# Tile numbers of the source stage read in smaller register loads, ranks kept in PSUM, and two loops with a fixed first slot

## The reference

```
h = relu(layernorm(x));  x = x + L0(h)     # attention: softmax over the edges of each node, weighted sum
h = relu(layernorm(x))
msg = relu(concat(h[src], h[dst], edge_attr) @ W1 + b1)
x = x + segment_sum(msg @ W2 + b2, src)    # summed by source node
```

## Time and profile before

| what | value |
|---|---|
| three executions, median (lowest to highest) | 5747.75 us (5745.49 to 5753.77) |
| the profiled execution | 5751.72 us, span in the profile 5749.9 us |
| mean granted clock of PE | 0.931 of full speed |
| PE busy | 5123.7 us, 89% of the span |
| DVE busy | 3965.7 us, 69% |
| ACT busy | 2966.4 us, 52% |
| POOL busy | 3885.3 us, 68% |
| chain that ended last | PE 57%, DMA 11%, issue 11%, POOL 9%, DVE 8% |
| source stage | 4378 to 5710 us, 107 turns |

### The profile page before, as it was taken

The page is one execution under the profiler, slowest core; times in us unless marked ns, Lnnn a source line. Parts: engine busy times, 40 slices in busy tenths (PEclk is TensorE's granted clock), DMA queues, the critical chain, the costliest instruction groups (busy, mean ns, idle before and its releaser), DMA issues.

```text
span 5749.9 us, 159286 instructions
## 1 busy us (share of the span) xinstructions
PE 5123.7 (89%) x33692; PEld 4028.2 (70%) x33693; DVE 3965.7 (69%) x14408; ACT 2966.4 (52%) x8485; POOL 3885.3 (68%) x3713
## 2 busy tenths in 40 slices
PE   4888888888888876999999999999997999999999
PEld 3677777777777764777666666666665777777777
DVE  6778788888778776555555555555455888888887
ACT  3566566666666553333333333332224777777776
POOL 4777777777777774777777777777775545545543
PEclk6888888888889887999999999999998999999999
DMA  4522222222222244999989989889996999999997
GB/s 109 163 53 53 53 53 54 53 53 53 53 53 53 53 127 130 281 271 266 260 256 265 257 256 263 263 235 282 253 257 176 214 210 213 212 211 214 212 212 188
DMA packets 859989, 990.83 MB, mean 172 GB/s; under 512 B 307993, under 2 KB 663225, under 8 KB 859775
## 3 DMA queue, kind: packets, MB, share of 16 engines
q1 hardware_dynamic: 662494, 608.23, 40.8%
q0 software_dynamic: 190592, 378.22, 24.6%
q10 hardware_dynamic: 6816, 3.38, 0.2%
HBM read 726.65 MB, written 262.76 MB: 172 GB/s over the span
## 4 chain that ended last, share of the span: by engine, by line
PE 57%; DMA 11%; issue 11%; POOL 9%; DVE 8%; DVEq 2%; ACT 2%; POOLq 0%; ACTq 0%; SPq 0%
PE bank L1703 13%; PE bank L1536 9%; PE bank L1626 8%; PE bank L1693 7%; PE bank L1628 7%; DMA xr<-arena 7%; POOL arena L498 4%; POOL xr L546 4%; PE bank L1462 2%; DMA arena<-h_tab,arena 2%; DVE arena L1054 2%; DVE arena L944 2%; PE bank L1616 2%; PE bank L1684 1%; DVEq L250 1%
## 5 line engine op out<-in xcount | busy, mean ns | idle before, releaser
L498 POOL DMA_INDIRECT arena<-h_tab,arena x1612 | 1563.8, 970 | 553.4 <-issue 408.4
L546 POOL DMA_INDIRECT xr<-arena x1612 | 1580.3, 980 | 511.9 <-issue 351.5
L1536 PE MATMUL bank<-arena 128*128 128x136 f32 x6448 | 1316.8, 333 | 73.3 <-DVE arena L1054 8.4
L718 ACT ACTIVATE arena<-bank 128x256 f32<-128x256 f32 x1612 | 593.3, 385 | 1400.8 <-PE bank L1628 923.3
L560 POOL DMA_INDIRECT arena<-p_tab,arena x428 | 666.8, 1558 | 667.1 <-DMA arena<-p_tab,arena 441.3
L1626 PE MATMUL bank<-arena 128*128 128x256 f32 x3224 | 1030.4, 402 | 91.5 <-ACT arena L718 50.5
L1536 PEld LDWEIGHTS bank<-arena 128*128 128x128 f32 x6448 | 987.1, 215 | 159.0 <-DVE arena L1054 63.2
L625 ACT ACTIVATE arena<-bank 128x256 bf16<-128x256 bf16 x1612 | 615.2, 382 | 808.1 <-PE bank L1462 727.6
L1628 PE MATMUL bank<-arena 128*128 128x256 f32 x3224 | 976.5, 385 | 0.0
L1703 PE MATMUL bank<-arena 128*128 128x257 f32 x3424 | 898.2, 384 | 4.2 <-ACT arena L795 2.2
L1054 DVE TENSOR_TENSOR arena<-arena,bank 128x272 f32 x1612 | 692.1, 429 | 188.8 <-PE bank L1536 160.2
(11 more groups left out here) (255 smaller groups left out, 6477.1 us busy)
## 6 DMA issues: line engine op xcount, KB each, us to landing
arena<-xr SPq DMA_DIRECT2D x428, 516.0 KB, 4.0
arena<-q_tab SPq DMA_DIRECT2D x1612, 128.0 KB
arena<-in_edge_attr SPq DMA_DIRECT2D x61, 832.0 KB, 8.8
arena<-rel_tab SPq DMA_DIRECT2D x124, 224.0 KB
arena<-h_tab,arena POOLq DMA_INDIRECT x1612
xr<-arena POOLq DMA_INDIRECT x1612
arena<-rel_tab SPq DMA_DIRECT2D x124, 192.0 KB
xr<-arena SPq DMA_DIRECT2D x26, 516.0 KB
```

What stands on the lines that cost most here:

```text
L498: pool.indirect_dma_start(G[:, q, t, :], None, h_tab, bass.IndirectOffsetOnAxis(ap=idx[:, q, t:t + 1], axis=0)).then_inc(sem(f"gath{q}"), 16)
L546: pool.indirect_dma_start(xr, bass.IndirectOffsetOnAxis(ap=pos[:, q, t:t + 1], axis=0), Rb[:, t, :], None).then_inc(sem(f"scat{m}"), 16)
L1536: last = pe.matmul(PSB[3 + t % 2][:, k * H * MW:(k + 1) * H * MW], OH[:, (t + 2 * q) % 4, k * P:(k + 1) * P], flat(msg[:, t, :, :]), start ...
```

## The change

In the source stage PE and DVE read the tile numbers differently. DVE still uses `pbrow`, but reads 8 columns a turn and not 12, and 4 for what stands behind its last turn. PE gets a second copy of the table, `pbrow1`, shifted so that the number of pair g stands in column g + 1: it reads 4 columns at m = 0 and 4 at m = 4 of each turn, from columns that are a multiple of 4, and a single one behind the loop. `pbrow1` lies where the row `d0row` of the target stage lay; SP loads it after its last load of that stage, and PE and DVE wait for both copies.

In the target stage `rank` on DVE adds `run0` in place, in PSUM, and `own` reads PSUM and writes `t49`; the bank is given back to PE by `own`, and no longer by `rank`.

DVE's and ACT's loops of the source stage begin at slot 0 of a block.

```diff
+        pbrow1 = Region(WORDS - NB * RB)([NPAIR + 16], I32, 1)
...
-        def pair_bins(engine, i):
+        def pair_bins(engine, row, first, count):
             return nc.values_load_multi_w_load_instructions(
-                pbrow[0:1, bass.ds(i * SB, SB + 4)], engines=[engine], min_val=0, max_val=NT - 1,
+                row[0:1, bass.ds(first, count)], engines=[engine], min_val=0, max_val=NT - 1,
...
             load_windows(NB - 1, 1, part=NT - 1)
-
+            sp.dma_start(pbrow1[:, 1:1 + NPAIR], pb_tab[0:NPAIR].rearrange("(a n) -> a n", a=1)).then_inc(sem("pb_in"), 16)
             sp.wait_ge(sem("main_done"), T)
...
-            with act.Fori(1, NTURN) as i:
+            with nc.Fori(1, NTURN, engines=[ENG.Activation], head_slot={ENG.Activation: 0}) as i:
                 sources(i)
...
             def rank(r, m):
-                V.tensor_tensor(t49[:, lo:hi, :], PSB[5][:, 0:(hi - lo) * NT].rearrange("p (t b) -> p t b", b=NT),
-                                run0.unsqueeze(1).to_broadcast([P, hi - lo, NT]), ALU.add).then_inc(sem("rk_used"), 1)
+                v = PSB[5][:, 0:(hi - lo) * NT].rearrange("p (t b) -> p t b", b=NT)
+                V.tensor_tensor(v, v, run0.unsqueeze(1).to_broadcast([P, hi - lo, NT]), ALU.add).then_inc(sem("run_added"), 1)
             def own(r, s, m):
-                dve.wait_ge(sem("rk_used"), 3 * r + m + 1)
-                V.tensor_tensor(t49[:, lo:hi, :], t49[:, lo:hi, :], oh49[:, s, lo:hi, :], ALU.mult).then_inc(sem("own_ready"), 1)
+                dve.wait_ge(sem("run_added"), 3 * r + m + 1)
+                V.tensor_tensor(t49[:, lo:hi, :], PSB[5][:, 0:(hi - lo) * NT].rearrange("p (t b) -> p t b", b=NT),
+                                oh49[:, s, lo:hi, :], ALU.mult).then_inc(sem("rk_used"), 1)
             def reduced(r):
-                dve.wait_ge(sem("own_ready"), 3 * r + 3)
+                dve.wait_ge(sem("rk_used"), 3 * r + 3)
...
-            dve.wait_ge(sem("pb_in"), 16)
+            dve.wait_ge(sem("pb_in"), 32)
...
             def sources(i, first=False, last=False):                    # DVE
-                regs = pair_bins(ENG.DVE, i)
+                regs = pair_bins(ENG.DVE, pbrow, SB * i, SB)
...
-            with dve.Fori(1, NTURN - 1) as i:
+            with nc.Fori(1, NTURN - 1, engines=[ENG.DVE], head_slot={ENG.DVE: 0}) as i:
                 sources(i)
             sources(NTURN - 1, last=True)
-            regs = pair_bins(ENG.DVE, NTURN)
+            regs = pair_bins(ENG.DVE, pbrow, NPAIR, 4)
...
             def sources(i, first=False):                                # PE
-                regs = pair_bins(ENG.PE, i)
                 for m in range(SB):
+                    if m % 4 == 0:
+                        regs = pair_bins(ENG.PE, pbrow1, SB * i + m, 4)
                     turnp(SB * i + m, m)
                     if not (first and m < 1):
-                        source_rows(SB * i + m - 1, (m - 1) % SB, regs[m + 3], first)
+                        source_rows(SB * i + m - 1, (m - 1) % SB, regs[m % 4], first)
...
-            pe.wait_ge(sem("pb_in"), 16)
+            pe.wait_ge(sem("pb_in"), 32)
...
-            regs = pair_bins(ENG.PE, NTURN)
-            source_rows(NPAIR - 1, SB - 1, regs[3], False)
+            regs = pair_bins(ENG.PE, pbrow1, NPAIR, 1)
+            source_rows(NPAIR - 1, SB - 1, regs[0], False)
```

## The result

The changed kernel takes 5705.26 us (median of 4 runs, 5700.23 to 5709.14) beside 5750.76 us for the kernel before in the same rounds (4 runs, 5745.49 to 5761.07). The ratio is 0.9918 with a 95% interval of [0.9901, 0.9935]: 47 us less, between 37 and 57. The forecast was 51 us less.

The account below looks back on a forecast made before the run. PE was taken to bound the source stage, losing 0.74 us around each turn's end. Terms -60 + 10 - 2 + 1 = -51 us gave 5697 us from a median of 5747.75; range 5672 to 5733 us.

Parts of the forecast that it names:

- PE at the turn's end: Source stage: PE's register load at each turn's end falls from 0.85 to 0.28 us; -60 us (bounds -74 to 0).
- The rival of a fixed price: A register load costs mostly the same whatever its count and PE pays twice; about 5745 us, no change; chance 0.11.
- Second load at m = 4: PE's new mid-turn load needs 0.47 us and slack covers 0.61, so nothing lost; 45 us lost at 0.85 us.
- The rival on the slower side: PE's second load at m = 4 comes uncovered, from 0.63 us a load on; 5778 us; chance 0.07.
- DVE's load: DVE's register load at the source turn's end falls from 0.85 to 0.57 us; alone worth 0, taken as 0.
- Late turns: Source turns delayed by chunk loads cost 14 us; shorter turns cut the four-buffer ring's slack; 24 us, so +10 (0 to +40).
- The rival that the ring takes +35 us: Source stage's ring of chunk buffers takes part of the gain, late turns growing by 35 us; 5723 us; chance 0.18.
- Ranks: Target stage: rank kept in PSUM leaves durations unchanged, may stop own slowing POOL's scatter; -2 us (-10 to +5).
- Loop heads: DVE's and ACT's source loops at a block's first slot: nothing won per turn, possible fetch miss on entry; +1 us (0 to +6).
- SP and waits: One more DMA on SP and the waits for both table copies, over before they are reached; 0 us.
- the marks set: Expected signs: PE loads 0.28 us, DVE 0.57, mean turn below 12.0, distance 2.1 across the end, 1.91 at m = 4, DMA 0.96.
- three signs of being wrong: Loads taking 0.5 us or more, L1347's waits for chunks doubling, or the target stage moving by over 10 us.

## Why the prediction was right

Direction and size held: -51 us forecast, -47 by the ratio and -42 between the two profiles. Two of its terms were too small, in opposite directions (+26 for +10, -9 for -2). That they cancelled in part, and that the sum came so near, is luck.

- *PE at the turn's end, -60 us.* Right in its mechanism and for the least turn, which fell from 12.30 to 11.74, 0.56 us x 106 = 59 us. Four registers cost 0.33 us at the floor rather than 0.28, and 0.45 in the median of the changed kernel. The mean load at the turn's head is 0.47 us after 0.91, so on all turns the load gave 47 us and not 59: 7 us of the difference are loads above their floor, counted below under the late turns, and 5 come from the offset, which is T - 0.15 with two loads of four and not T - 0.11. The rival of a fixed price falls: four registers cost 0.33 us, eight 0.60. The floor of about 600 ns that the Trainium skill gives in "DMA: Bandwidth & Descriptors", Latency and other measured facts, is not this trace's: 0.33 us. The prediction read the 200 ns per register of the Trainium skill ("Runtime: NRT & Kernel Launch", Instruction fetch mechanics) as a price for these loads. By its section Terms that page of the Trainium skill speaks of registers loaded from HBM. The loads here read SBUF, so the 71 ns of the earlier trace rows neither bears the figure out nor refutes it.
- *Second load at m = 4, nothing.* Right, and with more room than read from the earlier trace rows, about 0.9 us and not 0.61: the distance there is still 1.91 us. The rival on the slower side was real as a mechanism. The kernel with unaligned loads is that rival, at 20 us slower.
- *DVE's load, 0 alone and a wait of some 0.2 us a turn if PE alone were faster.* The second half was right (0.17 us by the ratios, 0.25 between two profiled executions). The first was mis-sized: alone it gives 7 us, out of late turns that were there before.
- *Late turns, +10.* This is the term that failed. The mean turn lies 0.37 us above the least instead of 0.13, so +26 us. Some 7 of them are not waiting at all: the mean load at the turn's head lies 0.13 us above its floor (0.47 and 0.33) instead of 0.06 (0.91 and 0.85), and the prediction had put the late turns down to chunk loads alone. For the other 19, the step behind it was "about 1 us of slack even in a turn of 11.7 us", from four buffers and a landing of 4.0 us. The buffers do not run freely: DVE's order ties each reload to the landing of a later chunk, a round of two chunks took 5.93 us in the place followed, and 11.6 to 12.1 us for two rounds, over the loop, leave no slack at 11.74. The rival that the ring takes +35 us was nearer in this one term, though not in the sum. Shown for the circuit: its rounds in the trace, and a chain without DMA once the chunks were lighter. That the order of DVE causes it is argued from the trace; the kernels with another order brought waits of their own and later landings, and so decide nothing about it. A limit in the DMA itself stands as the open rival.
- *Ranks, -2.* Mis-sized in the other direction: -9 us (-14 to -4), inside the stated bounds. The mechanism fits, POOL's scatters 980 to 973 ns in the mean and 11 us in sum. The step that failed is that POOL is "only one link of this stage's chain" and so hands on little: the stage from first to last scatter got shorter by those same 11 us, in the means of the nine traces with the edit and the five without.
- *Loop heads, +1.* Within the noise, -3 with an interval from -9 to +2.
- *SP and waits, 0.* No run shows anything of them.

In sum: -59 + 26 - 9 = -42 us between the profiles. Of the marks set, the loads of about 0.57 us on DVE (0.61) and the unchanged distance at m = 4 came true. The distance of 2.1 us across the end came true for the shortest turns only (2.27 in the median), and the loads of 0.28 us on PE took 0.33 at best. The mean turn below 12.0 did not come (12.11). The DMA share rose to 0.94, not 0.96. None of the three signs of being wrong appeared, but two came near: DVE's waits for chunks grew from 73 to 121 us, and the target stage moved by 8 us between the two profiles.

## What to carry to other kernels

When the bounding engine is made faster in a loop, work out the period of every circuit of buffers through the in-order engines, landing time included, and compare it with the new turn. Here 11.6 to 12.1 us met 11.74, the late turns took back 26 of 59 us (some 19 by waiting), and a further cut of PE's turn would meet the same circuit. Where two engines read the same numbers, measure the edits together as well as apart: alone they gave 14 and 7 us, together 32, more than the sum though not clear of the noise. Where an engine seldom waits for others through a stage, as POOL with its 1612 scatters, look for what lengthens its instructions: here 11 us off them were 11 us off the stage. And put tables that registers are loaded from where each load begins at a multiple of four words.

## What the runs showed of the hardware

- *The time of a register load goes by aligned groups of four.* From an aligned column, 4 registers take 0.33 us, 8 take 0.60 and 12 take 0.85: about 0.075 us and 0.26 for each group. A single register, behind PE's loop, takes 0.31 us, nearly as much as four. One column off the multiple of four, 4 registers take 1.00 us, 0.25 each. A reading that fits is that a whole group costs as much as one lone register: it gives the 26 registers of the earlier trace rows, six groups and two, 0.075 + 8 x 0.26 = 2.16 us (2.07 measured). Other offsets were not tried. Of SP's seven loads of 7 in the earlier trace rows only the first, from column 0, fits (1.15 us, one group and three); the others took 2.0 to 2.9 us, and why stays open.
- *A register load on PE costs the turn less than it takes*: T - 0.11 us at the turn's end with one load a turn (losses of 0.74 and 0.48 us at 0.85 and 0.59), T - 0.15 us with two (0.18 and 0.85 us at 0.33 and 1.00). In the middle of the turn, at m = 4, 0.33 us cost nothing and 1.00 us cost 0.30.
- *PE's loads of four are not always at their floor*: 0.45 us in the median in the changed kernel at a DMA share of 0.94, 0.335 with lighter chunks at 0.84. The share alone does not decide it: with DVE's loads split, and with DVE's new order as well, the medians are 0.348 and 0.337 us at 0.93, and with PE's loads alone 0.457 at 0.92. The cause stays open.
- *Moving one operand of DVE's multiplication from SBUF to PSUM* shortened it (598 to 592 ns) and shortened POOL's scatters by 11 us in sum; the longest scatter fell from 1.45 to 1.21 us. The addition ahead of it, which now also writes to PSUM, grew from 601 to 608 ns.
